# Head mixing's keys from demodulated weights: one product and one VectorE addition instead of a product, two ScalarE copies and a transpose

## The reference, cut to what matters

```python
def modulated_linear(x, s, aff_w, aff_b, w, b):          # one style per batch
    style = s @ aff_w.T + aff_b
    w_mod = w[None] * style[:, None, :]
    demod = rsqrt(sum(w_mod * w_mod, axis=2) + EPS)      # one number per batch and output column
    return einsum('bni,boi->bno', x, w_mod * demod[:, :, None]) + b

x1 = x + attention(modulated conv of x)                  # 32 batches x 128 tokens x 128 columns
kx = modulated_linear(x1, cond, k_aff_w, k_aff_b, k_w, k_b).reshape(32, 128, 16, 8)
out = softmax(kx @ kx.T / sqrt(8)) @ kx                  # per token, over its 16 heads
tok = modulated_linear(out, cond, o_aff_w, o_aff_b, o_w, o_b)
result = x1 + mixture_of_experts(tok)                    # 8 experts, top 2, a capacity
```

## Time and profile before

| what | us |
|---|---|
| median of 3 runs (516.62, 516.7, 518.55) | 516.7 |
| profiled execution's own time | 519.01 |
| its span, first to last instruction | 517.0 |
| PE busy (share of the span) | 499.2 (97%) |
| DVE busy | 401.2 (78%) |
| ACT busy | 371.2 (72%) |
| POOL busy | 324.0 (63%) |

### The profile page before, as it was taken

How to read it: one execution, slowest core, us unless ns; L and a number is a source line. 1 busy time by engine, 2 the same in 40 slices (tenths; PEclk the granted TensorE clock), 3 DMA queues, 4 the chain that set the end, 5 groups by cost and what they waited for, 6 DMA issues and landing times.

```text
span 517.0 us, 12870 instructions
## 1 busy us (share of the span) xinstructions
PE 499.2 (97%) x3896; PEld 348.6 (67%) x3896; DVE 401.2 (78%) x715; ACT 371.2 (72%) x851; POOL 324.0 (63%) x328
## 2 busy tenths in 40 slices
PE   7899999999999999999999999999999989889997
PEld 6866667666666777766676667666666756666664
DVE  4234788888888888888888888888888797736766
ACT  3467777777777777777777777777777437657873
POOL 1102677777777777777777777777777549004760
PEclk9999999999999999999999999999999989999999
DMA  6500000000000000000000000000000000000004
GB/s 221 155 1 2 2 1 2 1 0 0 0 0 0 0 0 0 0 0 0 0 0 0 0 0 0 0 0 0 0 0 2 1 1 0 2 0 2 0 21 143
DMA packets 9364, 7.19 MB, mean 14 GB/s; under 512 B 1088, under 2 KB 8832, under 8 KB 9216
## 3 DMA queue, kind: packets, MB, share of 16 engines
q1 hardware_dynamic: 9344, 6.94, 4.6%
HBM read 4.84 MB, written 2.10 MB: 13 GB/s over the span
## 4 chain that ended last, share of the span: by engine, by line
PE 89%; DVE 5%; issue 2%; ACT 2%; DMA 1%; SPq 1%; POOL 1%; DVEq 0%; ACTq 0%; POOLq 0%
PE bank_a L704 11%; PE misc L711 11%; PE bank_d L719 11%; PE bank_t L686 11%; PE bank_s L671 7%; PE bank_d L696 6%; PE bank_t L953 4%; PE bank_t L681 4%; PE misc L841 3%; PE misc L843 3%; PE misc L808 2%; PE bank_s L961 2%; PE bank_d L961 2%; PE misc L868 1%; PE bank_a L642 1%
## 5 line engine op out<-in xcount | busy, mean ns | idle before, releaser
L1374 POOL TENSOR_TENSOR pair<-kx 128x1152 f32<-128x1152 f32 x32 | 82.9, 2591 | 96.6 <-DVE shifted L422 77.7
L300 DVE TENSOR_REDUCE row_max<-bank_s 128x4 bf16<-128x512 f32 x128 | 89.4, 699 | 67.7 <-PE bank_s L671 67.7
L1339 POOL TENSOR_TENSOR mix_hi<-mix_hi 128x512 f32<-128x512 f32 (+2 forms) x96 | 79.7, 831 | 3.1
L1007 ACT ACTIVATE qT<-misc 128x512 f32<-128x512 f32 x64 | 39.1, 611 | 53.7 <-PE misc L711 53.6
L1007 ACT ACTIVATE prob<-bank_t 128x512 f32<-128x512 f32 x128 | 69.7, 603 | 4.4 <-PE bank_t L686 2.8
L719 PE MATMUL bank_d<-attT,wpost_sb 128*128 128x128 f32 x512 | 69.2, 278 | 0.2 <-DVE attT L308 0.2
L711 PE MATMUL misc<-yT,wq_sb 128*128 128x128 f32 x512 | 67.7, 275 | 0.0
L704 PE MATMUL bank_a<-prob,v 128*32 128x512 f32 x512 | 67.4, 598 | 0.0
L686 PE MATMUL bank_t<-qT,kT 64*128 64x256 f32 x512 | 65.7, 376 | 0.0
L1345 POOL TENSOR_TENSOR mix_hi<-weight,kx 128x1024 f32<-128x1024 f32 x32 | 63.1, 1973 | 0.3 <-ACT weight L1007 0.3
L711 PEld LDWEIGHTS misc<-yT,wq_sb 128*128 128x128 f32 x512 | 62.2, 192 | 0.8
(11 more groups left out here) (183 smaller groups left out, 934.9 us busy)
## 6 DMA issues: line engine op xcount, KB each, us to landing
out<-acc_all SPq DMA_DIRECT2D x8, 256.0 KB, 2.3
x_all<-in_xT SPq DMA_DIRECT2D x1, 1024.0 KB, 9.7
w_sb<-in_w SPq DMA_DIRECT2D x2, 512.0 KB
x_all<-in_xT SPq DMA_DIRECT2D x1, 768.0 KB, 7.6
wq_sb<-in_wq SPq DMA_DIRECT2D x1, 512.0 KB, 6.2
wpost_sb<-in_wpost SPq DMA_DIRECT2D x1, 512.0 KB, 9.8
x_all<-in_xT SPq DMA_DIRECT2D x1, 256.0 KB, 3.2
b_rows<-in_b SPq DMA_DIRECT2D x16, 4.0 KB
```

The costliest lines, as they stand in the source:

```text
L300: V.tensor_reduce(bass.AP(row_max, first_w * (P + 1) + HPG * p, [[HPG * P, P], [P + 1, 2], [KEY, 2], [1, 1]]), bank_s[:, :, :].rearrange(" ...
L1007: return nc.scalar.activation(out_, in_, func, **kw)
L1339: G.tensor_tensor(mix_hi[:, jd, 0:r, :], mix_hi[:, jd, 0:r, :], mix_hi[:, jd, r:2 * r, :], ALU.add).then_inc(s_hi, 1)
L1374: G.tensor_tensor(pair[:, :, :], bass.AP(kx2, jc * 2 * P, [[4 * P, P], [0, SHIFTS], [1, P]]), bass.AP(kx2, jc * 2 * P, [[4 * P, P], [MD, S ...
```

## The change

The keys' demodulation goes into the weights once, for all batches. POOL makes 32 diagonal matrices of `demod` in eight instructions (in the tile `acc_all`, which is unused until the end); PE multiplies the weights with them in eight products of 512 columns (`key_weights`), ACT copies the results over the diagonals. Then `keys(b)` swaps its operands: `x1s` is now the stationary one, and the output comes in rows of tokens. `keys_turned`, `keys_out` and ACT's `keys_twice` go; a `keys_twice` on DVE adds the bias and writes `kx2`. The weights and a bias row are loaded by two more DMAs. PE's wait for `wq` moves from before slot -2 to before the first queries, and fillers are placed anew.

```diff
 DVE
+                def keys_twice():
+                    dve.wait_ge(s_kx_mm, n(c))
+                    if s_is(c, 0):
+                        dve.wait_ge(s_ld_key, 32)
+                    need(dve, s_lo, 4 * (c - 2) + 1)
+                    need(dve, s_hi, 4 * (c - 2) + 1)
+                    need(dve, s_pair, n(c - 2))
+                    V.tensor_tensor(kx2[:, jc, :].rearrange("p (r f) -> p r f", r=2),
+                                    key_out(c).to_broadcast([P, 2, P]),
+                                    keyb_sb[:, :].unsqueeze(1).to_broadcast([P, 2, P]), ALU.add).then_inc(s_kx2, 1)
 DVE loop_slot
                         heads_max(a, 1)
+                    if C:
+                        keys_twice()
                     if D:
                         rows_joined()
 DVE drain_slot
                         weighted_rows()
+                        if C:
+                            keys_twice()
                         row_sum()
 SP, behind x_all, ahead of wpost
+            sp.dma_start(keyw_sb[:, :], key_w).then_inc(s_ld_key, 16)
+            sp.dma_start(keyb_sb[:, :], key_b.to_broadcast([P, P])).then_inc(s_ld_key, 16)
 PE
-            pe.wait_ge(s_ld_qkv, 48)
+            def key_weights(quads):
+                for q in quads:
+                    pe.wait_ge(s_ld_key, 32)
+                    pe.wait_ge(s_diag, q + 1)
+                    if q >= 5:
+                        pe.wait_ge(s_kw, q - 2)
+                    mm(bank_w[q][:, :, :], keyw_sb[:, :], acc_all[:, q * QUAD:(q + 1) * QUAD, :], start=True,
+                       stop=True, skip_group_check=True).then_inc(s_kw_mm, 1)
 PE keys(b)
-                    mm(key_out(b)[:, 0, :], modw_sb[:, 1, :], x1s[:, :], start=True, stop=True).then_inc(s_kx_mm, 1)
-                def keys_turned(b): ...
+                    mm(key_out(b)[:, 0, :], x1s[:, :], acc_all[:, bass.ds(b, 1), :].rearrange("p a f -> p (a f)"),
+                       start=True, stop=True).then_inc(s_kx_mm, 1)
 PE loop_slot, in its order
                     if s_is(s, -1):
-                        keep_going(8)
+                        keep_going(20)
+                        pe.wait_ge(s_ld_qkv, 48)
 ...                                              slot 0, ahead of scores_t(s, j, 0)
-                        keep_going(5)
+                        key_weights((4, 5))
+                        pe.wait_ge(s_kw, 2)
 ...                                              behind keys(c)
+                    if s_is(s, 0):
+                        key_weights((6,))
 ...                                              behind scores_t(s, j, 1)
                     if s_is(s, -1):
-                        keep_going(6)
+                        key_weights((0,))
+                    if s_is(s, 0):
+                        key_weights((7,))
 ...                                              behind the product of xs
-                    if C:
-                        keys_turned(c)
                     if A:
                         scores(a, ja, 1)
                     if s_is(s, -1):
-                        keep_going(6)
+                        key_weights((1, 2, 3))
                     if B:
...
+                        if s_is(s, 0):
+                            pe.wait_ge(s_kw, QUADS)
                         denominators(s)
 ACT
-                def keys_out(): ...              with its calls
-                def keys_twice(): ...            with its calls
+                def key_weights(quads):
+                    for q in quads:
+                        act.wait_ge(s_kw_mm, q + 1)
+                        f(acc_all[:, q * QUAD:(q + 1) * QUAD, :], bank_w[q][:, :, :]).then_inc(s_kw, 1)
...      slot -1: (0,) behind v, (1, 2, 3) behind y_raw; slot 0: (4, 5) behind narrow_q, (6,) behind v, (7,) behind copy_q(a, ja, 1)
 POOL, end of slot -1
+                    pool.wait_ge(s_demod, 5)
+                    for q in range(QUADS):
+                        G.tensor_tensor(acc_all[:, q * QUAD:(q + 1) * QUAD, :],
+                                        ident[:, :].unsqueeze(1).to_broadcast([P, QUAD, P]),
+                                        demod[:, 1, q * QUAD:(q + 1) * QUAD].unsqueeze(2).to_broadcast([P, QUAD, P]),
+                                        ALU.mult).then_inc(s_diag, 1)
```

More of the change, by code:

```diff
@@ L36, with build @@
 LOOP_FROM, LOOP_TO = 4, BATCH - 2
-def build(nc, xT, condT, aff_wT, aff_b, mod_wT, mod_b, wq, wk, wv, wpost, gate_wT,
+def build(nc, xT, condT, aff_wT, aff_b, mod_wT, mod_b, key_w, key_b, wq, wk, wv, wpost, gate_wT,
           w1, b1T, w2, b2, out):
@@ L68, in build @@
         modb_sb = sb("modb_sb", [P, 3])
+        keyw_sb = sb("keyw_sb", [P, P])
+        keyb_sb = sb("keyb_sb", [P, P])
         wq_sb = sb("wq_sb", [P, HEADS * KEY])
@@ L167, in key_out @@
             return misc[1][:, 0:1, :] if s_is(b, BATCH - 1) else bank_x[1][:, 0:1, :]
+        bank_w = bank_t + [bank_d] + [bank_x[0], bank_x[1], bank_d, bank_x[0], bank_x[1]]
         def mix_out(b):
@@ L794, in keys @@
                     pe.wait_ge(s_x1s, n(b))
-                    mm(key_out(b)[:, 0, :], modw_sb[:, 1, :], x1s[:, :], start=True, stop=True).then_inc(s_kx_mm, 1)
-                def keys_turned(b):
-                    pe.wait_ge(s_kxT, n(b))
-                    nc.tensor.transpose(key_out(b)[:, 0, :], kxT[:, :], ident[:, :]).then_inc(s_kxn_mm, 1)
+                    if s_is(b, 0):
+                        pe.wait_ge(s_kw, QUADS)
+                    mm(key_out(b)[:, 0, :], x1s[:, :], acc_all[:, bass.ds(b, 1), :].rearrange("p a f -> p (a f)"),
+                       start=True, stop=True).then_inc(s_kx_mm, 1)
                 def mixing_turned(b):
@@ L1149, in drain_slot @@
                         ahead_relu(0)
-                        keys_out()
                         ahead_relu(1)
-                        keys_twice()
                         head_weights()
@@ L1204, in slot @@
                       misc[0][:, 2:4, :].rearrange("p a (g e) -> p (a g) e", e=KEY)).then_inc(s_v, 1)
-                if C:
-                    keys_out()
+                if s_is(s, -1):
+                    key_weights((0,))
+                if s_is(s, 0):
+                    key_weights((6,))
                 if B:
@@ L1404, in _ @@
                                 ALU.add).then_inc(s_added, 1)
-_INS = ("xT", "condT", "aff_wT", "aff_b", "mod_wT", "mod_b", "wq", "wk", "wv", "wpost", "gate_wT",
+_INS = ("xT", "condT", "aff_wT", "aff_b", "mod_wT", "mod_b", "key_w", "key_b", "wq", "wk", "wv", "wpost", "gate_wT",
         "w1", "b1T", "w2", "b2")
```

4 lines of the change are left out of this document (3 added, 1 removed).

## The result

The changed kernel took 523.07 us (median of 4 executions, 521.68 to 524.50), the kernel before beside it 516.66: ratio 1.0116, interval [1.0075, 1.0156]. Timed again later beside the kernel before: 524.25 (6 executions) against 517.93, ratio 1.0111 [1.0092, 1.0131]. It is slower by about 6 us. The profiled execution took 522.1, its span is 520.3 (before: 519.01 and 517.0).

A forecast was written before the change was run, and what follows sets the result against it. PE bounds the kernel now; after the change a ring through DVE and POOL would. Loop +2.9, start +1.9 and end -1.1 sum to +3.7, added to the median 516.7: 520.4 us, slower, range 513.5 to 525.5.

The forecast's parts named there:

- First queries, -2.0: Start: with the `wq` wait moved, the first queries begin at about 13.3 instead of 15.26, gaining 2.0 us.
- L868 runs at about 8.7: Start on PE: L868 no longer waits for `wq` until 11.39; forty passes follow without a break, taking 4.5 us.
- Rival 2: Start: the forty fillers run at the lower clock (+3.2 us) or key weights land late; 523.6 us, chance 0.12.
- Key products and ACT's last copy, +3.1 + 0.8: Start: eight products cost 6.9 us against 3.8 of fillers removed; PE's wait for ACT's last copy adds 0.8.
- Loop, +2.9: Loop: 27 slots each grow by 0.12 us, +3.2, less 0.3 gained up to slot 3.
- The ring: Loop: dependency cycle through DVE and POOL, starting at PE's group 1 scores; takes 12.34 us a slot, exceeding PE's 12.11.
- The addition's 0.34: Loop on DVE: `keys_twice` between group 1's maximum and `rows_joined` adds 0.34 us start to start, bounds 0.20 and 0.61.
- the wait ahead of T: Loop: from group 0's next maximum to T, the start of PE's group 1 scores (L671); 0.10 us, bounds 0.05 and 0.33.
- the 10.68 from S to the end of the next maximum: Loop: from S, the start of `shifted`, to the end of group 0's next maximum; 10.68 us, moving whole with S.
- DVE shows no idle time: Loop: from `mix_lo` to the next slot's group 0 maximum, DVE was read as running without idle time.
- End, -1.1: End, slot 31: POOL's sums finish before `pick_ahead`, returning 1.0 us, and the dropped transpose returns 0.1.
- rival 3: End: earlier `pair` in slot 32 also removes PE's 1.2 us wait for `mixed`; 519.2 us, chance 0.09.

The follow-up runs named there:

- gap: Changed kernel with DVE's key addition moved ahead of the row maximum of group 1, into DVE's idle time; 518.86 us, ratio 1.0030 to the kernel before.
- rows: Changed kernel with the addition in DVE's idle time, twelve products of ones ahead of the counts, and key weights made without the eight key products; 516.09 us, ratio 0.9963.
- doubled: Changed kernel with DVE's key addition made twice in its place in the loop, once into a spare tile; 533.72 us, ratio 1.0302.
- early: Kernel before with only the wait for `wq` moved to the first queries, twenty filler products ahead of it; 518.89 us, ratio 1.0034.
- start_only: Changed kernel's start, with the keys of every batch made the old way as in the kernel before; 523.72 us, ratio 1.0114.
- early_warm: Kernel before with the wait for `wq` moved to the first queries, plus twelve products of ones ahead of PE's wait for the counts; 517.27 us, ratio 0.9991.
- best: Changed kernel with the addition in DVE's idle time, ACT's last key-weight copy ahead of `copy_q`, and twelve products of ones ahead of the counts; 516.34 us, ratio 0.9964.
- after: The changed kernel itself, first measurement and profile; 523.07 us, ratio 1.0116 to the kernel before.
- after, again: The changed kernel unaltered, timed and profiled again beside the kernel before; 524.25 us, ratio 1.0111.

## Why the prediction was right, and where it was not

The forecast was 520.4, slower, range 513.5 to 525.5. Slower was right, the time is 2.7 above. Its four terms against the two profiles, +3.7 against +3.26:

- **First queries, -2.0: right in one execution, gone in the other.** 13.45 in the first profile (13.3 said), -1.65. Part of the difference is that I read the queries of the kernel before at 15.26, the end of the last filler; they start at 15.10. But the wait for `wq` was cover. Behind it an early stretch of slow passes didn't matter (10.98 is still ahead of 11.39); without it the queries follow that stretch, at 15.67, +0.57. My step "L868 runs at about 8.7" took one execution's start for every execution's; six of the ten timed executions are in the upper group, 2.2 to 2.4 above the lower. Rival 2 had slow fillers as its mechanism, but in the forty passes; those ran at 4.63 in both profiles, it was the fourteen ahead of L905.
- **Key products and ACT's last copy, +3.1 + 0.8: right.** +4.11; the products take 7.39 from start to start and the fillers that they replace took 3.93, +3.5, and the wait is 0.73. POOL's diagonals (12.53 to 20.56) and the loads hid as said: PE waits for neither.
- **Loop, +2.9: mechanism right, size wrong.** +0.25. The ring was said to take 12.34 and takes 12.23. The addition's 0.34 is 0.32 and the wait ahead of T is 0.06, not 0.10; the term that was mis-sized is the 10.68 from S to the end of the next maximum, which is 10.60. The step behind it that failed is "DVE shows no idle time". The part in which POOL and DVE hold each other did move with S, as said: S to `x_all`, behind `mix_lo`, is 6.09 before (251.15 to 257.24) and 6.09 after (253.71 to 259.80), and on the mean of twenty slots 6.08 or 6.09 in all 13 profiles. `normalise` comes later (2.27 behind S, before 2.19) and `mix_lo` starts 0.06 later, but `mix_lo` then takes 1.31 instead of 1.37 and ends at the same distance. The Trainium skill, "SBUF — State Buffer", section "Who interferes with whom", on which the forecast took 12.34 rather than 12.25, calls the shared ports an exclusive lock; the 1.07 and 1.08 behind `mix_hi` agree. What shrank is the last step, `h_max` to the maximum: 0.57 before, 0.51 after, 0.57 again in gap. Before, that maximum starts 0.05 behind the end of PE's scores of group 0 (260.69 + 0.39 = 261.08, 261.13): DVE waited for PE there, although the row has no idle time in brackets. On the mean of twenty slots it starts 0.04 behind them and 0.57 behind `h_max` in the eight kernels in which PE is the bound, 0.30 to 0.34 and 0.51 in the five in which the ring is. So a little of PE's slot was counted into the ring. Over 27 slots an error of 0.11 is 3 us.
- **End, -1.1: right up to the counts, then lost.** -0.56 and -0.55. The product in `pick_ahead` gives 0.83, with its neighbours 1.57 (1.0 said); rows and doubled, whose clock stays up in slot 31, need 20.36 and 20.41 to `not_ahead`, so about 0.9 of the gain was lost to a fall of the clock there (to 0.50 between 416 and 418). PE's wait of 1.2 for `mixed` stays (1.21), against rival 3, and a second of 0.71 joins it, as POOL's instructions now run beside `mix_sum` and `mix`. Then the fall behind the counts takes 1.66. No term had these, and in before's profile both stretches ran at 1.00.

So the errors (loop 2.65 too high, the fall behind the counts 1.66 and the start 0.56 too low) cancel in part, and that the sum meets the profiles to 0.4 is luck in that measure. The rest of the medians' difference, 6.4 against 3.1 between the profiled executions, is that the changed kernel's profile was of its lower group (522.1 against 523.07) and before's profile 2.35 above its median. Why the latter was slow isn't settled: its clock fell to 0.50 between 422 and 424, at the end of PE's wait of 2.5 us for `ahead_w`, but the column around it (33.40) is only 0.31 longer than the 33.09 of early and start_only, which have no fall there.

Open too: why the early passes stay slow for longer in some executions, and why the times of early_warm's twelve and best's five form no upper group.

## What to carry to other kernels

Before weights are made ready ahead of a loop to save an instruction in it, price both on the engine that bounds the kernel: here eight products of 0.86 against 31 transposes of 0.11, and the saving was lost even so, as the replacement stood in the next engine's ring; moved by one instruction into that engine's idle time it cost nothing. A wait that is taken away at the start may have been covering something that varies from run to run, so go by more than one execution. And the price of a setup is worth another look when the array is a quarter used: products with 32 rows each ran four at a time.

## What the runs showed of the hardware that was not expected

- Early passes of TensorE at 0.24 us and 0.13 us stand under the same granted clock of 1.00 in the profile (2 us from 6.00 hold 10 passes in one execution and 20 in the other). The ratio is about that of the two levels of 1.2 and 2.4 GHz, so the column does not show the clock of the first microseconds. The list of clock levels in the trace agrees: its first entry, full clock, stands at 5.24 us in after and at 9.97 in after, again, and the column counts what lies ahead of it as 1.00. In the three profiles with the late first queries that entry comes at 9.5 to 10.0, in the eight others with the wait moved at 3.9 to 5.5. The Trainium skill, "TensorE: Matmul & The Clock Gate", section "Part 1: The HAM clock gate", says that the number of slow products at a kernel's start varies from run to run; the two profiles agree.
- The clock fell to its lower level behind 2.24 us of idle TensorE in six of nine profiles and in none of four in which products of ones filled that time. It also fell in slot 31, where PE was busy without a break (in best 0.68, 0.50 and 0.96 from 410 to 416), in seven of the nine profiles with the new keys; there `not_ahead` came after 21.2 to 21.6 us, in the two others, rows and doubled, after 20.4. The keys alone don't decide it: two of the four with the old keys, start_only and early_warm, have it too (22.45 and 22.29, the others 21.80 and 21.78). Ahead of it PE had run the gate's products of 8 columns each. What sets it off in slot 31 was not tried.
